# The six-layer stage of an eight-stage transformer kernel: scores of a unit put ahead of the previous unit's values on TensorE, and three norms applied by GpSimd

## Chip, core and metric

One NeuronCore of a Trainium2 chip runs the whole program in one launch. The metric is the device time of that launch in microseconds, taken over several executions. The kernel before takes 5420.99 us (median of 3; 5419.63 to 5421.79).

## What is computed

The input is `x` of 8 batches x 256 tokens x 128 features in fp32, with a condition vector per batch and a context of 64 tokens per batch. Eight blocks follow one another, each added to `x`. The change is in the fifth, which is six layers of this (16 heads of 8 features, feed-forward width 512):

```python
for i in range(6):
    xn = _adaln(x, noise_emb, n1_w[i], n1_b[i])          # layer norm, then a gain and a shift
    q, k, v = split(xn @ qkv_w[i].T); q, k = _rope(q), _rope(k)
    x = x + _attn(q, k, v, src_mask) @ so_w[i].T         # 256 keys
    xn = _adaln(x, noise_emb, n2_w[i], n2_b[i])
    q = _rope(xn @ cq_w[i].T); k = _rope(context @ ck_w[i].T); v = context @ cv_w[i].T
    x = x + _attn(q, k, v, ctx_mask) @ co_w[i].T         # 64 keys
    xn = _adaln(x, noise_emb, n3_w[i], n3_b[i])
    x = x + (gelu(xn @ f1_w[i].T + f1_b[i]) @ f2_w[i].T + f2_b[i])
```

where `_ln(x) = (x - m) * rsqrt(v + eps)` has the mean and variance of a token's 128 features. The part that the change moves to GpSimd is this subtraction and scaling.

## The kernel before

**The stage.** `dit_layers` keeps the tokens in SBUF as four pairs of batches (512 tokens, 4 tiles of 128). `course(slots)` runs one software-pipelined list of 26 **slots**; every pair in every layer is one slot for its own attention. In slot n the attention over the pair's own tokens runs, together with the cross attention of the pair of slot n-1, the feed-forward of the pair of slot n-2, and the norm, queries, keys and values of the pair of slot n+1. A slot without some of these is shorter: the first slot has no attention, the next two have no feed-forward, the last three end what is open. 21 slots have every part.

**The units.** A slot has 12 steps k = 0 to 11, each with one **unit** of attention: k = 0 to 7 are own units (one batch, four heads, 256 keys, so two exponentials of 128x1024), k = 8 to 11 are cross units (one exponential). A unit has

- group maxima: `max_scores(u, g)`, g = 0 to 3, bf16 matmuls (L1904 in the profile) into one of two PSUM banks used in turn; VectorE takes the row maximum of each (`row_max`, L2299), `turn_max` turns them on TensorE (L1916), and VectorE's `place_max` (L2317) makes the fp32 queries of the unit with the maximum in a spare feature;
- scores: `scores(u, 0)` and `scores(u, 1)` (L1942 own, L1946 cross) into PSUM banks 0 to 3;
- the exponentials on ScalarE (L2175), out of these banks into `probs`;
- values: `values(u)`, 8 matmuls (L1968 own, L1971 cross) into bank 4, which also make the sums; ScalarE copies the bank (`copy_values`, L2186), `turn_values` turns it on TensorE (L1980), and VectorE inverts the sums (L2329) and multiplies (L2339, `normalise`).

**The order.** There is no scheduler: each engine's program is written out, and engines wait for each other by semaphores. In step k of unit u TensorE does, outside the feed-forward's place (k = 7):

```python
values(u-1); scores(u, 0); max_scores(u+1, 2); scores(u, 1)
max_scores(u+1, 3); max_scores(u+2, 0); chain_early; turn_values(u-1)
turn_max(u+1); max_scores(u+2, 1); chain_late
```

`scores(u, 0)` waits for `queries_ready` of u (that is `place_max(u)`) and for all exponentials of u-1. `max_scores` waits until the row maximum of the group two places before it is taken, since there are two banks. `values(u-1)` waits for the exponentials of u-1 and for `normalise(u-2)`. VectorE does in the same step:

```python
row_max(u+1, 1); chain_early; row_max(u+1, 2); row_max(u+1, 3)
row_max(u+2, 0); chain_late; invert_sums(u-1); normalise(u-1); place_max(u+1)
```

ScalarE does `copy_values(u-1)`, the exponentials of u, `chain`. The `chain_early`, `chain_late` and `chain` functions hold the projections, norms and feed-forward of the neighbouring pairs, spread over the steps: on TensorE the turned norms (L1986), the 512-column projections (L1990) and by-token projections (L1994, L2007); on VectorE the statistics of a norm (`stats`, k = 0, 2 and 4, late in the last two), the applied norm (`apply`, L2354, four instructions in k = 1, 3 and 5, early), rotations (L2360) and residual sums (L2370). In step k = 7 TensorE does the four 512-column products of the feed-forward's first half (L2001) with `values(u-1)` between them, and the scores last.

GpSimd does the inverse roots of the norms (`root`, L2134 and L2137) and four sums a slot.

## Time and profile before

| What | Value |
|---|---|
| Runs | 5419.63, 5420.99, 5421.79 us |
| Span of the profiled execution, first to last instruction | 5413.8 us |
| Own time of the profiled execution, outside the profile | not recorded; the span is 7.2 us below the median of the runs |
| Granted TensorE clock, whole span | 0.918 of full speed |
| TensorE matmuls busy, of the span | 4614.7 us (85%) |
| VectorE busy | 2884.4 us (53%) |
| ScalarE busy | 2082.3 us (38%) |
| GpSimd busy | 576.5 us (11%) |
| The changed stage's exponentials | 2117.97 to 3915.2 us of the span |

The page gives busy time by engine over the whole program. The stage that the change touches lies in the middle third. A busy share does not say which engine sets the pace of a step, because TensorE's matmuls are pipelined and four of them share the array in most of these lines; the timeline and the words in its brackets (how long an engine was idle before an instruction, and which instruction ended that) do. In the timeline, instructions of one line are merged, so that "x3" and 1.95 us are three row maxima from the first start to the last end.

### The profile page before, as it was taken

Reading aid. Unit: us, or ns where it says so; the run is one execution under the profiler, and the core shown is the slowest. Engines: PE = TensorE matmul, PEld = TensorE weight load, DVE = VectorE, ACT = ScalarE, POOL = GpSimd, SP = SyncE. Lnnn points to the kernel's source line nnn. Section 1 sums busy time; section 2 is a strip of 40 time slices with the busy share of each in tenths; the row PEclk is TensorE's granted clock in tenths of the full one; section 3 lists DMA queues with packets and bytes.
Section 4 is the critical chain, followed back from the end, with each engine's and each line's share of the span. In section 5 each row is a group of like instructions: output and inputs, shape, how many; then the busy total and the mean of one; then the engine's idle time right before and its main releaser. Section 6 shows DMA issues by size and latency. Waiting matters only on the chain. (4 is left out here: it accounts for less than half of the span.)

```text
span 5413.8 us, 111310 instructions
## 1 busy us (share of the span) xinstructions
PE 4614.7 (85%) x45206; PEld 3112.5 (57%) x45501; DVE 2884.4 (53%) x9511; ACT 2082.3 (38%) x4120; POOL 576.5 (11%) x1302
## 2 busy tenths in 40 slices
PE   5489999999999965889989889899778979788784
PEld 3357777777777753555555555555444756566463
DVE  6634555555555535777766677666455224433433
ACT  2223333333333312665665666566433322212221
POOL 3300111111111112111111111111000000000000
PEclk8789999999999976999999999999889989878786
DMA  0000000000000011000000000000010010000000
GB/s 26 23 18 2 2 2 2 2 2 2 2 2 2 2 61 54 4 4 6 7 6 4 4 9 4 6 1 1 1 40 1 1 44 1 1 1 1 1 1 9
DMA packets 32272, 49.22 MB, mean 9 GB/s; under 512 B 8244, under 2 KB 23638, under 8 KB 31136
## 3 DMA queue, kind: packets, MB, share of 16 engines
q1 hardware_dynamic: 28448, 38.27, 2.2%
q8 instruction: 366, 6.00, 0.4%
q10 hardware_dynamic: 2304, 2.11, 0.1%
q0 software_dynamic: 1024, 1.78, 0.1%
q14 instruction: 130, 1.06, 0.1%
HBM read 37.72 MB, written 4.19 MB: 8 GB/s over the span
## 5 line engine op out<-in xcount | busy, mean ns | idle before, releaser
L2299 DVE TENSOR_REDUCE l_m<-psum 128x2 bf16<-128x512 f32 x768 | 503.8, 692 | 148.8 <-PE psum L1904 146.5
L2175 ACT ACTIVATE l_probs<-psum,l_mcol 128x1024 f32<-128x1024 f32 x384 | 406.3, 1109 | 159.2 <-PE psum L1942 159.2
L1184 PE MATMUL psum<-g_gx,ident 128*128 128x128 f32 x1536 | 416.0, 389 | 18.0
L1173 PE MATMUL psum<-g_still,ident_bf 128*128 128x256 bf16 (+3 forms) x1551 | 391.5, 281 | 1.7 <-PEq L58 1.7
L1904 PE MATMUL psum<-l_kb,l_qmb 32*128 32x256 bf16 x1536 | 295.4, 273 | 56.1 <-DVE l_m L2299 52.4
L1252 ACT ACTIVATE g_th<-g_pre 128x256 f32<-128x256 f32 x512 | 191.7, 417 | 314.3 <-DVE g_pre L1285 314.3
L1184 PEld LDWEIGHTS psum<-g_gx,ident 128*128 128x128 f32 x1536 | 279.4, 195 | 12.8
L1942 PE MATMUL psum<-l_qm,l_keys 32*128 32x256 f32 x3072 | 265.1, 418 | 13.3 <-issue 13.3
L2186 ACT COPY l_heads_out<-psum 128x256 f32<-128x256 f32 (+1 forms) x292 | 130.0, 445 | 369.8 <-PE psum L1968 186.3
L1285 DVE TENSOR_TENSOR g_pre<-g_encp,psum 128x256 f32<-128x256 f32 x512 | 192.8, 418 | 132.9 <-PE psum L1202 122.4
L2299 DVE TENSOR_REDUCE l_cm<-psum 128x4 bf16<-128x256 f32 x400 | 166.0, 427 | 179.8 <-PE psum L1904 179.6
L1968 PE MATMUL psum<-l_probs,l_v 128*32 128x256 f32 x3072 | 220.8, 408 | 46.7 <-DVE l_o L2339 29.1
L1187 PEld LDWEIGHTS psum<-g_shares,g_crows 128*128 128x128 f32 x1536 | 197.0, 189 | 78.9 <-issue 78.9
L1942 PEld LDWEIGHTS psum<-l_qm,l_keys 32*128 32x128 f32 x3072 | 180.5, 191 | 101.8 <-issue 94.1
L1173 PEld LDWEIGHTS psum<-g_still,ident_bf 128*128 128x128 bf16 x1808 | 224.3, 136 | 12.5 <-issue 2.3
L1187 PE MATMUL psum<-g_shares,g_crows 128*128 128x8 f32 x1536 | 212.8, 245 | 17.6
L1179 PE MATMUL psum<-g_encw,g_attnT 128*32 128x128 f32 x6144 | 220.8, 277 | 0.0
L3430 ACT ACTIVATE l_probs<-psum 128x1024 f32<-128x1024 f32 x80 | 81.9, 1023 | 326.1 <-PE psum L3257 228.7
L1904 PEld LDWEIGHTS psum<-l_kb,l_qmb 32*128 32x128 bf16 x1536 | 112.1, 93 | 164.0 <-DVE l_m L2299 75.2
L1256 ACT COPY g_crows<-psum 128x128 f32<-128x128 f32 x256 | 67.9, 265 | 348.3 <-PE psum L1179 348.3
L1270 POOL TENSOR_SCALAR g_kept<-g_zh 128x8 f32<-128x8 f32 x256 | 59.6, 233 | 1321.2 <-DVE g_zh L1311 1321.2
L1179 PEld LDWEIGHTS psum<-g_encw,g_attnT 128*32 128x32 f32 x6144 | 152.2, 109 | 67.7 <-DVE g_attnT L1293 67.7
(567 smaller groups left out, 9761.9 us busy)
## 6 DMA issues: line engine op xcount, KB each, us to landing
s_w<-in_S_w SPq DMA_DIRECT2D x16, 256.0 KB, 5.0
f_w<-in_F_w SPq DMA_DIRECT2D x2, 2048.0 KB, 12.5
l_wf<-in_L_W SPq DMA_DIRECT2D x6, 576.0 KB, 3.8
l_w<-in_L_W SPq DMA_DIRECT2D x1, 3072.0 KB, 10.6
l_nw<-in_L_nw SPq DMA_DIRECT2D x1, 2304.0 KB, 8.0
l_wc<-in_L_W SPq DMA_DIRECT2D x6, 384.0 KB, 3.0
h_w<-in_H_W ACTq DMA_DIRECT2D x16, 129.0 KB, 3.0
h_w<-in_H_W SPq DMA_DIRECT2D x16, 129.0 KB, 3.0
```

Of the source, the lines that this page charges most:

```text
L1173: pe.matmul(psum[:, bank, 0:cols], cst["ident_bf"][:], still[:, 0:cols], start=True, stop=True)
L1179: last = pe.matmul(psum[32 * p:32 * p + 32, bank, 0:D], attnT[:, 2 * p:2 * p + 32], encw[:, p, gate, :], start=True, stop=True)
L1184: pe.matmul(psum[:, bank, 0:P], cst["ident"][:], repeated(gx(gate, s)), start=True, stop=False)
L1187: pe.matmul(psum[:, bank, 0:B], crows[:, i, :], shares[:], start=False, stop=True)\
L1252: act.activation(th[:, i, :, :], pre[:, i, :, :], ACT.Tanh).then_inc(sig["tanh_ready"], 1)
L1285: dve.tensor_tensor(pre[:, i, :, :], encp[:, i, :, :], query[:, i, :].unsqueeze(2).to_broadcast([P, PAIRS, C]), ALU.add)\
L1904: last = pe.matmul(psum[:, bank, x.width * t:x.width * (t + 1)], queries, far_keys, start=True, stop=True)
L1942: last = pe.matmul(psum[:, g, S * part:S * part + S], keys[group(g), s.buf, x.j % 2, S * x.b + P * part:S * x.b + P * part + P], qm[group( ...
L1968: last = pe.matmul(psum[group(g), VALUES, 0:S], v[:, s.buf, 2 * x.b + part, GROUP * g + x.j, :], probs[:, u % 2, part, S * g:S * g + S], s ...
L2175: act.activation(probs[:, u % 2, chunk, :].rearrange("p (g n) -> p g n", g=GROUP), psum[:, 0:GROUP, S * chunk:S * chunk + S], ACT.Exp, bia ...
L2186: act.copy(heads_out[:, u % 2, 0:cols], psum[:, VALUES, 0:cols]).then_inc(sig["values_copied"], 1)
L2299: dve.tensor_reduce(place, psum[:, c.bank(("max", u, g)), 0:x.tiles * x.width] .rearrange("p (t k) -> p t k", t=x.tiles), AX.X, ALU.min)\
```

## The change

On TensorE `values(u-1)` goes from the front of a step to a place behind `scores(u, 1)`, in all steps but k = 7. On ScalarE `exponentials(u, 0)` goes ahead of `copy_values(u-1)`, so that the copy stands between an own unit's two exponentials, and behind a cross unit's only one. The three `apply` calls leave VectorE; GpSimd makes them directly behind its inverse root, with a wait until the previous contents of the buffer have been turned.

```diff
                             else:
-                                values(done)
                                 scores(u, 0)
                                 max_scores(after, 2)
                                 scores(u, 1)
+                                values(done)
                                 max_scores(after, 3)
                                 max_scores(later, 0)
                                 chain_early(s, i, k)
...
+                def apply(pool, n, w, pair, done, dst):
+                    pool.wait_ge(sig[n + "_rstd_ready"], done + 1)
+                    if done:
+                        pool.wait_ge(sig[n + "_turned"], done)
+                    for t in range(PT):
+                        last = pool.tensor_scalar(dst[:, t, :], Y[:, PT * pair + t, :], w["mv"][:, t, 0:1],
+                                                  w["rstd"][:, t, :], ALU.subtract, ALU.mult)
+                    last.then_inc(sig[n + "_normed"], 1)
...
                             root(pool, "n2", n2, nx)
+                            apply(pool, "n2", n2, s.mid_pair, nx, xn[1])
...
                             root(pool, "n1", n1, nn)
+                            apply(pool, "n1", n1, s.next_pair, nn, xn[0])
...
                             root(pool, "n3", n3, nf)
+                            apply(pool, "n3", n3, s.late_pair, nf, xn[2])
...
                             if u is not None:
+                                exponentials(u, 0)
                                 if not (k == FF_PLACE and s.ff):
                                     copy_values(c.behind(u))
-                                exponentials(u, 0)
                                 if units[u].own:
                                     exponentials(u, 1)
...
                         if k == 1 and s.context:
-                            apply("n2", n2, s.mid_pair, nx, xn[1])
...
-                        if k == 3 and s.following:
-                            apply("n1", n1, s.next_pair, nn, xn[0])
...
-                        if k == 5 and s.ff:
-                            apply("n3", n3, s.late_pair, nf, xn[2])
```

TensorE, the second own step of the first slot with attention (k = 1): `l_probs,l_v` are the values, `l_qm,l_keys` the scores, `l_kb,l_qmb` the group maxima.

```order
 L2058 MATMUL psum<-l_wc,l_ctxT 128x128
-L1968 MATMUL psum<-l_probs,l_v 32x256 x8
-L1942 MATMUL psum<-l_qm,l_keys 128x256 x4
-L1904 MATMUL psum<-l_kb,l_qmb 128x256 x2
-L1942 MATMUL psum<-l_qm,l_keys 128x256 x4
+L1942 MATMUL psum<-l_qm,l_keys 128x256 x4
+L1904 MATMUL psum<-l_kb,l_qmb 128x256 x2
+L1942 MATMUL psum<-l_qm,l_keys 128x256 x4
+L1968 MATMUL psum<-l_probs,l_v 32x256 x8
 L1904 MATMUL psum<-l_kb,l_qmb 128x256 x4
 L1980 MATMUL psum<-ident,l_heads_out 128x128 x2
```

The values have passed the scores, and now stand between them and four group-maximum matmuls (those of group 3 of the next unit and of group 0 of the one after).

TensorE, the first cross step (k = 8) of the same slot: here the projection of the next pair's values (`l_wa,l_xn1T`) stands between the group maxima and the turned values (`ident,l_heads_out`, outside the piece).

```order
 L1990 MATMUL psum<-l_xn1T,l_wa 128x512
-L1968 MATMUL psum<-l_probs,l_v 32x256 x8
-L1946 MATMUL psum<-l_qm,l_ckeys 64x256 x4
-L1904 MATMUL psum<-l_ckb,l_cqmb 128x64 x4
-L1946 MATMUL psum<-l_qm,l_ckeys 64x256 x4
+L1946 MATMUL psum<-l_qm,l_ckeys 64x256 x4
+L1904 MATMUL psum<-l_ckb,l_cqmb 128x64 x4
+L1946 MATMUL psum<-l_qm,l_ckeys 64x256 x4
+L1968 MATMUL psum<-l_probs,l_v 32x256 x8
 L1904 MATMUL psum<-l_ckb,l_cqmb 128x64 x8
 L1994 MATMUL psum<-l_wa,l_xn1T 128x128 x4
```

The same move, and the turned values of this step are behind the values, two groups and the projection.

GpSimd, one slot with feed-forward, as it stands with the change: `l_xn<-l_y` are the applied norms (L2144), and every other row was there before in this order.

```order
L2134 TENSOR_SCALAR l_n_veps<-l_n_mv 128x4
L2137 TENSOR_TENSOR l_n_rstd<-l_n_veps,mhalf 128x4
L2144 TENSOR_SCALAR l_xn<-l_y,l_n_mv,l_n_rstd 128x128 x4
L2162 TENSOR_TENSOR l_cqT<-l_tc 128x512
L2134 TENSOR_SCALAR l_n_veps<-l_n_mv 128x4
L2137 TENSOR_TENSOR l_n_rstd<-l_n_veps,mhalf 128x4
L2144 TENSOR_SCALAR l_xn<-l_y,l_n_mv,l_n_rstd 128x128 x4
L2168 TENSOR_TENSOR l_y<-l_y,l_constf 128x512
L2173 TENSOR_TENSOR l_qT<-l_t 128x512
```

The four instructions of each norm went in behind the inverse root; nothing else of this queue changed its place.

## Rows read from the trace of the kernel before

**Rows 1.** the page: its line of the span

```profile
span 5413.8 us, 111310 instructions
```

**Rows 2.** the timeline, ScalarE: exponentials; start us, us, engine line op out<-in xcount [idle before <-releaser]

```profile
2242.94 2.12 ACT L2175 ACTIVATE l_probs<-psum,l_mcol 128x1024 f32<-128x1024 f32 x2 [0.70 <-PE psum L1942]
...
2387.84 2.12 ACT L2175 ACTIVATE l_probs<-psum,l_mcol 128x1024 f32<-128x1024 f32 x2 [0.70 <-PE psum L1942]
...
2397.87 2.12 ACT L2175 ACTIVATE l_probs<-psum,l_mcol 128x1024 f32<-128x1024 f32 x2 [0.91 <-PE psum L1942]
...
2404.05 2.12 ACT L2175 ACTIVATE l_probs<-psum,l_mcol 128x1024 f32<-128x1024 f32 x2 [0.91 <-PE psum L1942]
...
2421.29 2.12 ACT L2175 ACTIVATE l_probs<-psum,l_mcol 128x1024 f32<-128x1024 f32 x2 [0.90 <-PE psum L1942]
...
2437.43 1.11 ACT L2175 ACTIVATE l_probs<-psum,l_mccol 128x1024 f32<-128x1024 f32 x1 [1.03 <-PE psum L1946]
...
2442.16 1.11 ACT L2175 ACTIVATE l_probs<-psum,l_mccol 128x1024 f32<-128x1024 f32 x1 [0.82 <-PE psum L1946]
...
2460.28 2.12 ACT L2175 ACTIVATE l_probs<-psum,l_mcol 128x1024 f32<-128x1024 f32 x2 [0.70 <-PE psum L1942]
...
3788.01 2.12 ACT L2175 ACTIVATE l_probs<-psum,l_mcol 128x1024 f32<-128x1024 f32 x2 [0.70 <-PE psum L1942]
```

**Rows 3.** the timeline of the second own step of a slot, all engines

```profile
2390.58 1.07 PE L1968 MATMUL psum<-l_probs,l_v 128*32 128x256 f32 x16
...
2391.58 0.92 PE L1942 MATMUL psum<-l_qm,l_keys 32*128 32x256 f32 x10
...
2392.13 0.27 PE L1904 MATMUL psum<-l_kb,l_qmb 32*128 32x256 bf16 x1
...
2392.54 1.95 DVE L2299 TENSOR_REDUCE l_m<-psum 128x2 bf16<-128x512 f32 x3 [0.31 <-PE psum L1904]
...
2392.67 0.38 PE L1904 MATMUL psum<-l_kb,l_qmb 32*128 32x256 bf16 x2
...
2393.38 0.37 PE L1904 MATMUL psum<-l_kb,l_qmb 32*128 32x256 bf16 x2 [0.34 <-DVE l_m L2299]
...
2394.40 0.20 DVE L2329 RECIPROCAL l_rsum<-psum 128x8 f32<-128x8 f32 x1
...
2394.78 0.47 DVE L2317 SCALAR_TENSOR_TENSOR l_qm<-l_qT,l_narrow,psum 128x256 f32<-128x256 f32 x1
...
2395.45 1.07 PE L1968 MATMUL psum<-l_probs,l_v 128*32 128x256 f32 x16
```

**Rows 4.** the timeline, VectorE, fifth own step: the statistics of a norm, and an applied norm

```profile
2411.50 0.86 DVE L2345 BATCH_NORM_STATS2 l_n_stats<-l_y 128x6 f32<-128x128 f32 x4
...
2412.70 0.18 DVE L2329 RECIPROCAL l_rsum<-psum 128x8 f32<-128x8 f32 x1
...
2414.20 1.12 DVE L2354 TENSOR_SCALAR l_xn<-l_y,l_n_mv,l_n_rstd 128x128 f32<-128x128 f32 x4
```

**Rows 5.** the timeline around the eighth step and the ninth

```profile
2437.59 1.16 PE L1994 MATMUL psum<-l_wa,l_xn1T 128*128 128x128 f32 x8
...
2439.01 0.21 DVE L2329 RECIPROCAL l_rsum<-psum 128x8 f32<-128x8 f32 x1 [0.62 <-PE psum L1980]
...
2439.39 0.74 DVE L2317 SCALAR_TENSOR_TENSOR l_qm<-l_cqT,l_narrow,psum 128x512 f32<-128x512 f32 x1
```

**Rows 6.** the timeline of the first step of the course: queries placed, scores behind them

```profile
2114.89 0.47 DVE L2317 SCALAR_TENSOR_TENSOR l_qm<-l_qT,l_narrow,psum 128x256 f32<-128x256 f32 x1
...
2115.41 1.65 PE L1942 MATMUL psum<-l_qm,l_keys 32*128 32x256 f32 x10
```

**Rows 7.** groups of instructions of GpSimd, shapes apart: busy us, mean ns | idle before us

```profile
L2146 POOL TENSOR_TENSOR l_ckT<-l_tk 128x128 f32<-128x128 f32 x25 | 11.3, 454 | 85.6 <-DVE l_tk L2360 85.6
```

**Rows 8.** windows: us, busy and (x) of PE, PEld, DVE, ACT, POOL, PEclk, DMA, GB/s

```profile
2387.80:2460.30 72.50, 65.03 (x679) 37.96 (x678) 51.92 (x136) 45.07 (x64) 9.23 (x12) 1.00 0.03 7
...
2912.90:2920.80 7.90, 6.84 (x51) 3.01 (x50) 6.16 (x21) 3.78 (x7) 1.21 (x2) 0.78 0.00 0
```

More of the change, by code:

```diff
@@ L2349, in stats @@
                         last.then_inc(sig[n + "_var_ready"], 1)
-                    def apply(n, w, pair, done, dst):
-                        dve.wait_ge(sig[n + "_rstd_ready"], done + 1)
-                        for t in range(PT):
-                            last = dve.tensor_scalar(dst[:, t, :], Y[:, PT * pair + t, :], w["mv"][:, t, 0:1],
-                                                     w["rstd"][:, t, :], ALU.subtract, ALU.mult)
-                        last.then_inc(sig[n + "_normed"], 1)
                     def rotated(projected, done, table, first, cols, dst, name=None):
```

## The prediction

> **What bounds the kernel now.** The page gives one profiled execution with a span of 5413.8 us [rows 1], 7.2 us under the median of the runs; I work out a difference from that execution and add it to the median. Its shares of busy time name TensorE, but they do not say what ends a step, so the views I use are the starts of the exponentials, which give the length of each step, and then the timeline of single steps with the words on idle time.
>
> A full slot runs from exponential to exponential in 2460.28 - 2387.84 = 72.44 us [rows 2], and TensorE is busy in 65.03 of such 72.50 us at full clock [rows 8]: at most 7.5 us a slot are idle. From 2242.94 to 3788.01 lie 21 full slots and 1545.07 us, while 21 x 72.44 is 1521.2. The 24 us over it are steps at a lower granted clock: the window of one such step 2 is 7.90 us long with a clock of 0.78 (a mean over it of TensorE's two levels, 1.2 and 2.4 GHz) [rows 8], where the same step takes 2404.05 - 2397.87 = 6.18 us undisturbed [rows 2]. What ends an undisturbed step is seen in the second own step [rows 3]: values start at 2390.58, scores 1.00 later at 2391.58, the group maximum inside them at 2392.13; VectorE starts three row maxima at 2392.54, 0.96 after the scores began, and is done with them and at the inversion at 2394.40; 0.38 later it places the next queries, which takes 0.47. The next values start at 2395.45. So the loop is values, scores, exponentials or row maxima, values. The placed queries are ready at 2395.25, 1.2 us before the next scores start (values 1.00 behind 2395.45): they have slack, because values stand between them and the scores.
>
> **What the change removes and adds.** Count every time from the start S of a unit's scores.
>
> *Values behind the scores.* The 1.00 us before S goes from the loop. In its place the values take TensorE from S+1.09 (2392.67 - 2391.58 [rows 3]) to S+2.09. Behind them stands the group maximum 3, which used to start at S+1.09. VectorE needs 0.41 from its start to the row maximum (2392.13 to 2392.54), so it begins the third row maximum at S+2.50, where it now is at S+1.58, right behind the one before. Two row maxima of 0.6 bring it to S+3.70. Then come the late vector work of the step, 0.38 from inversion to placing, 0.47 of placing, and 0.05 until the scores start (2114.89 + 0.47 to 2115.41 [rows 6]). **The new floor of an own step is 4.60 us plus the late vector work**, and nothing stands between placing and scores any more. The exponentials are not what waits longest: they begin 1.42 after the scores (2397.87 against 2395.45 + 1.00) and take 2.12 [rows 2, 3], so even with a copy of 0.5 between them they end at S+4.04. The turned values are shorter too in an own step: their copy ends by S+3.0, and turning takes less than half a microsecond. So the values leave one loop and delay another by almost as much.
>
> *Step by step.* (Durations without a group are from the same timeline, one slot of it.) Own steps 0 and 1: TensorE's late projection or turn ends them, at 5.09 and 4.80; together 9.89 against 2397.87 - 2387.84 = 10.03 [rows 2]: -0.14. Step 2: late statistics of 1.20 (2411.50 to 2412.70 [rows 4]), less 0.03 of inversion gap: 5.77. Step 3: the second cross query projection starts at S+2.71, its rotation frees the bank 1.85 later, and the by-token projection of 1.08 follows: 5.70. Step 4: statistics again, 5.77. Step 5: a rotation that ends the vector chain 1.45 after its start at S+3.88: 5.38. Together 22.62 against 2421.29 - 2397.87 = 23.42 [rows 2]: -0.80. Steps 6 and 7: the key projection waits for a rotation that comes 0.59 later than now, and the feed-forward behind it is TensorE work back to back, so +0.59; then the scores of step 8 need only the exponentials of step 7, where now the 1.00 of values stands behind the same event: -0.41 together. Step 8: values to S+2.40 (cross scores take 1.40), two maxima 0.29, the value projection 1.00, turned values; the inversion came 1.42 after that projection began (2437.59 to 2439.01 [rows 5]), so now at S+4.11; placing 0.38 later takes 0.74; scores at 5.28, against 2442.16 - 2437.43 = 4.73 [rows 2]: +0.55. Step 9: two halves of the feed-forward keep TensorE busy throughout, and moving 1.00 us inside it changes nothing. Step 10 has step 8's pattern: +0.57. Step 11: residual sum and placing behind a projection that starts 1.00 later, less the values: +0.25. Sum: -0.14 - 0.80 - 0.41 + 0.55 + 0.57 + 0.25 = **+0.02 us a slot, under +1 us over 21**.
>
> *The norms.* VectorE loses 12 instructions a slot, 1.12 us for each four [rows 4]. They stand early in steps 1, 3 and 5. Under the new order VectorE has 0.9 us idle before the third row maximum, so what goes there goes from idle time; only step 3 would have been late by 0.2 with it, and 5.70 already has it out. GpSimd's price is not in the trace: from below VectorE's 0.28 an instruction (1.12 for four), from above its two-input sum of the same size, 0.454 [rows 7], so 1.1 to 1.8 us for four; I take 1.8, the same engine. TensorE reads the tightest of the three, the third norm, some 4.2 us after its inverse root is ready, so 1.8 is hidden, and twice that would be. Nothing is queued behind it on GpSimd that is wanted soon. Uncovered it is only in the first slot and the last two, where no attention runs: three times 0.4 to 0.7, about +1.2. On this the Trainium skill speaks against the change: its page "GPSIMD Engine Reference", section "Engine selection", puts elementwise work on VectorE and calls GpSimd about twice as slow for two inputs, near line rate for one. The trace agrees in direction, 0.454 on GpSimd [rows 7] against 0.28 on VectorE [rows 4] for the same size, and by that rule the sum would stay as it is, since the work is covered.
>
> *The ends.* Two slots without feed-forward lose the gains of steps 2 and 7 and lose 0.9 in step 9, whose turned values no longer hide behind anything: +1.4 each, +2.9. The last three cross steps outside full slots: +1.5.
>
> Total: 0.4 + 1.2 + 2.9 + 1.5 = +6 on 5421.0: **5427 us, no change within 0.2%** (0.2%, 11 us, is about what a measurement of this kernel tells from no change).
>
> **Bounds.** The 0.05 between placing and scores may be 0.15, as between a row maximum (ended 2393.23) and the group maximum behind it (2393.38 [rows 3]); with six such steps a slot that is 0.6 x 21 = +13 us. Values behind scores instead of behind other matmuls could overlap by 0.05 or cost 0.07, their last drain (1.07 against 1.00): -6 to +9 in the same steps. I keep 0.05 and 1.00, the rows of those same instructions.
>
> **Rivals.**
>
> *A, faster by the clock (0.17).* The 24 us of low clock [rows 2, 8] lie in steps 2 and 4 of some slots. There TensorE waits longest; the new order shortens steps 2 and 3 by 0.8 together. If the clock then stays up: 5427 - 24 = 5403 us. Against it: step 4 still has 1.5 us of wait.
>
> *B, the loop pays in full (0.06).* If the row maxima were not the next bound and each full slot lost half of its 7.5 idle us, it would be 5421 - 21 x 3.7 = 5343. I do not believe in it since the two banks forbid it; half of that, 5380, if values and group maxima overlap.
>
> *C, slower by the clock (0.16).* Steps 8, 10 and 11 get a wait of about 1 us each, where TensorE now has next to none. A low-clock step costs about 7.9 - 6.2 = 1.7 us; if one more falls in every second slot, 21 x 0.5 x 1.7 = +18, so 5445 us. It decides once the granted clock drops in cross steps. The Trainium skill's page "TensorE: Matmul & The Clock Gate", section "HAM oscillation — how this bites in real kernels", says that repeated waits throttle TensorE again and again; here that would give this rival its time.
>
> *D, slower by hand-over (0.18).* The 0.15 above instead of 0.05, or the values' 0.07: 5427 + 13 = 5440 us. What decides is the time from placing to scores.
>
> That the change does not do what it says is excluded by the listed order on both engines.
>
> **How the numbers follow.** The forecast holds 0.43. Faster is A and B, 0.23; slower is C and D, 0.34, and same is 0.43. The predicted time is 5427. The range goes from A, 5403, rounded to 5402, to above C with D's half, 5450: it leaves out B and the case that C and D both hold, under 0.2.
>
> **What would show it.** In the changed profile: step lengths near 5.8 in steps 2 and 4, 5.3 in steps 8 and 10, and 15.6 for 6 and 7 together; scores whose wait is ended by the placed queries (the place where now values wait for the exponentials or the normalised output); VectorE idle 0.9 before the third row maximum; GpSimd busier by 80 to 130 us (73 norms at 1.1 to 1.8) with no TensorE wait on it except at the ends. It is wrong if own steps other than 6 fall below 4.6, if scores wait for exponentials in most steps, or if the clock in the stage's window is not near 0.97.

## The result, and the profile after

| | Before | After |
|---|---|---|
| Median of 12 runs each | 5421.14 us (5398.09 to 5440.68) | 5432.78 us (5425.10 to 5458.32) |
| Ratio to before, runs on the same chip compared | | 1.0038 (1.0023 to 1.0053) |
| Span of the profiled execution | 5413.8 us | 5425.1 us |
| First to last exponential of the stage | 1796.1 us | 1820.3 us |

The ratio is that of executions at the faster of two speeds; of all executions in this document one, of e4 below (6022.59 us at a granted clock of 0.712), was at the slower and is left out.

The change makes the kernel slower by 0.38%. The time lies inside the range that was given, but the sign is not that of the likeliest case, which was no change within 0.2%. By the medians the loss is 11.6 us, by the ratio, which compares runs on the same chip, 20.6 us; the stage itself, from its first exponential to its last, lost 24.2 us in the profiled execution. The rest of the profile is not touched by the change and moved by itself: behind the stage 1499.7 us before and 1484.1 us after, and between 1478 and 1505 us over the eleven kernels measured here. So below I judge each kernel by the stage and by the ratio, and take neither from a single span.

The page after: its span, busy times and four of its groups.

```profile
span 5425.1 us, 111380 instructions
...
PE 4591.5 (85%) x45206; PEld 3065.6 (57%) x45501; DVE 2809.6 (52%) x9219; ACT 2064.2 (38%) x4120; POOL 805.0 (15%) x1594
...
L2311 DVE TENSOR_REDUCE l_m<-psum 128x2 bf16<-128x512 f32 x768 | 515.9, 692 | 251.1 <-PE psum L1904 249.7
...
L1942 PE MATMUL psum<-l_qm,l_keys 32*128 32x256 f32 x3072 | 265.2, 415 | 86.3 <-DVE l_qm L2329 72.3
...
L1904 PE MATMUL psum<-l_kb,l_qmb 32*128 32x256 bf16 x1536 | 243.4, 280 | 25.9 <-DVE l_m L2311 24.4
...
L2144 POOL TENSOR_SCALAR l_xn<-l_y,l_n_mv,l_n_rstd 128x128 f32<-128x128 f32 x292 | 229.3, 798 | 7.6
```

Both parts of the change are to be seen. GpSimd has 229.3 us of applied norms, 798 ns each, and TensorE's own scores (L1942) now sit idle for the placed queries (the line numbers of ScalarE, and of VectorE up to the place where it applied the norm, are 12 higher than before: placing is L2329, inversion L2341, exponentials L2187; behind that place they are 5 higher, rotations L2365). VectorE is less busy, 2809.6 us against 2884.4, and waits more for the group maxima of own units (251.1 us, where it was 148.8). The view of the line of the own scores gives their idle times, of weight loads and matmuls together, and how often each cause ended one:

```profile
its engine sat idle before it (us, times) until:
  DVE l_qm L2329: 189.1, 192
  issue: 32.7, 51
```

The starts of the exponentials give the steps, as before [rows 2]. These are of one slot with the clock up throughout:

```profile
2399.83 1.11 ACT L2187 ACTIVATE l_probs<-psum,l_mcol 128x1024 f32<-128x1024 f32 x1 [2.64 <-PE psum L1942]
...
2410.06 1.11 ACT L2187 ACTIVATE l_probs<-psum,l_mcol 128x1024 f32<-128x1024 f32 x1 [0.28 <-PE psum L1942]
...
2416.05 1.11 ACT L2187 ACTIVATE l_probs<-psum,l_mcol 128x1024 f32<-128x1024 f32 x1 [2.34 <-PE psum L1942]
...
2449.05 1.11 ACT L2187 ACTIVATE l_probs<-psum,l_mccol 128x1024 f32<-128x1024 f32 x1 [1.68 <-PE psum L1946]
...
2454.27 1.11 ACT L2187 ACTIVATE l_probs<-psum,l_mccol 128x1024 f32<-128x1024 f32 x1 [1.64 <-PE psum L1946]
...
2472.66 1.11 ACT L2187 ACTIVATE l_probs<-psum,l_mcol 128x1024 f32<-128x1024 f32 x1 [2.64 <-PE psum L1942]
```

The slot takes 2472.66 - 2399.83 = 72.83 us, where it took 72.44: +0.39, with +0.02 forecast. Step 2 is 2416.05 - 2410.06 = 5.99, step 8 is 2454.27 - 2449.05 = 5.22. The table has the undisturbed lengths of all steps, in us, of the kernels that matter most (the experiments e2, e3 and e8 come below):

| Step | 0 | 1 | 2 | 3 | 4 | 5 | 6+7 | 8 | 9 | 10 | 11 | slot |
|---|---|---|---|---|---|---|---|---|---|---|---|---|
| before | 5.16 | 4.88 | 6.18 | 6.04 | 5.61 | 5.59 | 16.15 | 4.72 | 7.70 | 4.83 | 5.59 | 72.44 |
| forecast | 5.09 | 4.80 | 5.77 | 5.70 | 5.77 | 5.38 | 15.74 | 5.28 | 7.70 | 5.40 | 5.84 | 72.47 |
| after | 5.25 | 4.97 | 5.99 | 5.75 | 5.99 | 5.42 | 15.84 | 5.22 | 7.47 | 5.27 | 5.65 | 72.83 |
| e3 | 5.06 | 4.49 | 5.57 | 5.72 | 5.50 | 5.39 | 15.84 | 5.43 | 7.68 | 5.48 | 5.86 | 72.01 |
| e8 | 5.06 | 4.49 | 5.57 | 5.72 | 5.51 | 5.39 | 15.84 | 5.06 | 7.69 | 4.76 | 5.86 | 70.94 |

Where the forecast failed is seen in one own step with the clock up, all engines (some instructions left out):

```profile
2403.67 0.92 PE L1942 MATMUL psum<-l_qm,l_keys 32*128 32x256 f32 x10
...
2404.42 0.61 PE L1942 MATMUL psum<-l_qm,l_keys 32*128 32x256 f32 x5
...
2404.96 1.07 PE L1968 MATMUL psum<-l_probs,l_v 128*32 128x256 f32 x16
...
2405.96 0.39 PE L1904 MATMUL psum<-l_kb,l_qmb 32*128 32x256 bf16 x4
...
2406.39 1.30 DVE L2311 TENSOR_REDUCE l_m<-psum 128x2 bf16<-128x512 f32 x2 [0.95 <-PE psum L1904]
...
2407.59 0.20 DVE L2341 RECIPROCAL l_rsum<-psum 128x8 f32<-128x8 f32 x1
...
2407.96 0.47 DVE L2329 SCALAR_TENSOR_TENSOR l_qm<-l_qT,l_narrow,psum 128x256 f32<-128x256 f32 x1
...
2408.64 0.92 PE L1942 MATMUL psum<-l_qm,l_keys 32*128 32x256 f32 x10
...
2412.57 0.86 DVE L2357 BATCH_NORM_STATS2 l_n_stats<-l_y 128x6 f32<-128x128 f32 x4
...
2414.11 0.47 DVE L2329 SCALAR_TENSOR_TENSOR l_qm<-l_qT,l_narrow,psum 128x256 f32<-128x256 f32 x1
...
2414.64 0.92 PE L1942 MATMUL psum<-l_qm,l_keys 32*128 32x256 f32 x10 [0.46 <-DVE l_qm L2329]
...
2415.34 3.14 POOL L2144 TENSOR_SCALAR l_xn<-l_y,l_n_mv,l_n_rstd 128x128 f32<-128x128 f32 x4
```

The scores start at S = 2403.67. The values start at 2404.96, S+1.29, and end for the next instruction at 2405.96, S+2.29. I had them at S+1.09 and S+2.09, since the group maximum 3 stood at S+1.09 in that place before [rows 3]. The row maxima therefore start at 2406.39, S+2.72 instead of S+2.50. From there everything is as forecast: the inversion 1.20 later, placing 0.37 behind it, and, in the next step, behind its own placing, scores at 2414.64, 0.06 after the end of placing (2414.11 + 0.47). The values themselves cost 1.00, as before.

The granted clock is the other part. Windows over this slot, and over one step 5 that fell low:

```profile
2399.83:2472.66 72.83, 64.31 (x682) 36.48 (x682) 48.87 (x124) 44.11 (x63) 18.63 (x23) 1.00 0.03 7
```

```profile
2500.60:2508.20 7.60, 7.60 (x51) 3.72 (x50) 3.59 (x9) 4.06 (x6) 3.72 (x5) 0.58 0.00 0
```

The first window has TensorE at 2.4 GHz throughout. In the second the mean granted clock is 0.58, so most of it ran at 1.2 GHz, and the step took 2508.64 - 2500.90 = 7.74 us instead of 5.42; TensorE was busy all the time. What TensorE did before it fell is in the first of these rows, a wait of 1.53 us for placed queries in step 4; the second is the same instruction in the undisturbed slot, where the clock stayed up behind the same wait:

```profile
2499.21 0.92 PE L1942 MATMUL psum<-l_qm,l_keys 32*128 32x256 f32 x10 [1.53 <-DVE l_qm L2329]
...
2426.37 0.92 PE L1942 MATMUL psum<-l_qm,l_keys 32*128 32x256 f32 x10 [1.53 <-DVE l_qm L2329]
```

Added up over the 21 full slots, 71.7 us lie at the low level, where it was 51.2 us; after, it falls late in step 4 of 16 slots and lasts into step 5, where it was in step 2 of six and step 4 of nine. The five slots without it are every fourth, from the 3rd to the 19th, so the fall comes in a fixed order; what sets that order no run tells.

The 24.2 us of the stage come out as: 21 slots with 0.39 each, +8.2; low clock in them, +6.0 (1559.26 against 1545.06 us for the 21, less 8.2); the slots ahead of them +5.5; those behind them +4.5. The clock's part is of one execution each.

### The profile page after: what moved, and what is told of

It reads as the page before. It is cut to its first block and busy times, and to the rows that moved or that the text cites. A ratio compares the mean times of both kernels' runs of the same rounds, so it can differ in the third digit from the quotient of the medians.

```text
span 5425.1 us, 111380 instructions
## 1 busy us (share of the span) xinstructions
PE 4591.5 (85%) x45206; PEld 3065.6 (57%) x45501; DVE 2809.6 (52%) x9219; ACT 2064.2 (38%) x4120; POOL 805.0 (15%) x1594
## 5 line engine op out<-in xcount | busy, mean ns | idle before, releaser
L2311 DVE TENSOR_REDUCE l_m<-psum 128x2 bf16<-128x512 f32 x768 | 515.9, 692 | 251.1 <-PE psum L1904 249.7
L2187 ACT ACTIVATE l_probs<-psum,l_mcol 128x1024 f32<-128x1024 f32 x384 | 426.1, 1116 | 295.9 <-PE psum L1942 295.9
L1942 PE MATMUL psum<-l_qm,l_keys 32*128 32x256 f32 x3072 | 265.2, 415 | 86.3 <-DVE l_qm L2329 72.3
L1904 PE MATMUL psum<-l_kb,l_qmb 32*128 32x256 bf16 x1536 | 243.4, 280 | 25.9 <-DVE l_m L2311 24.4
L1942 PEld LDWEIGHTS psum<-l_qm,l_keys 32*128 32x128 f32 x3072 | 177.7, 187 | 147.8 <-DVE l_qm L2329 116.8
L2144 POOL TENSOR_SCALAR l_xn<-l_y,l_n_mv,l_n_rstd 128x128 f32<-128x128 f32 x292 | 229.3, 798 | 7.6
L2187 ACT ACTIVATE l_probs<-psum,l_mccol 128x1024 f32<-128x1024 f32 x100 | 111.4, 1114 | 254.4 <-PE psum L1946 254.4
L3430 ACT ACTIVATE l_probs<-psum 128x1024 f32<-128x1024 f32 x80 | 81.9, 1024 | 309.1 <-PE psum L3257 228.7
```

The source lines that it names most:

```text
L1904: last = pe.matmul(psum[:, bank, x.width * t:x.width * (t + 1)], queries, far_keys, start=True, stop=True)
L1942: last = pe.matmul(psum[:, g, S * part:S * part + S], keys[group(g), s.buf, x.j % 2, S * x.b + P * part:S * x.b + P * part + P], qm[group( ...
L2144: last = pool.tensor_scalar(dst[:, t, :], Y[:, PT * pair + t, :], w["mv"][:, t, 0:1], w["rstd"][:, t, :], ALU.subtract, ALU.mult)
L2187: act.activation(probs[:, u % 2, chunk, :].rearrange("p (g n) -> p g n", g=GROUP), psum[:, 0:GROUP, S * chunk:S * chunk + S], ACT.Exp, bia ...
L2311: dve.tensor_reduce(place, psum[:, c.bank(("max", u, g)), 0:x.tiles * x.width] .rearrange("p (t k) -> p t k", t=x.tiles), AX.X, ALU.min)\
```

## The experiments

Each kernel is the changed one or the one before with one edit. In diffs the places are those of the quoted order of TensorE, ScalarE and VectorE. The summary first; "low clock" is the time at the lower level in the 21 full slots, "stage" is first to last exponential, both of one profiled execution, and the ratio is to the kernel before. The low clock of one execution is not the order's alone: before and e1 have the same slot and differ by 10 us in it, e3, e7 and e8 have the same steps 0 to 5 and 13.7, 20.5 and 30.7 us, and the mean granted clock of 31 executions of the kernel before on one chip lay between 0.914 and 0.926. So differences of 10 or 20 us in that column tell nothing.

| Kernel | Slot, us | Low clock, us | Stage, us | Ratio |
|---|---|---|---|---|
| before | 72.44 | 51.2 | 1796.1 | 1 |
| after | 72.83 | 71.7 | 1820.3 | 1.0038 (1.0023 to 1.0053) |
| e1 norms alone | 72.45 | 61.4 | 1808.0 | 1.0007 (0.9986 to 1.0028) |
| e2 order alone | none undisturbed | 88.7 | 1833.3 | 1.0064 (1.0040 to 1.0087) |
| e3 group maximum 3 ahead of the values | 72.01 | 13.7 | 1781.9 | 0.9956 (0.9935 to 0.9977) |
| e4 placing early | 72.80 | 0 | 1779.6 | 0.9975 (0.9951 to 0.9998) |
| e5 copy ahead of exponentials | 73.30 | 81.9 | 1838.3 | 1.0098 (1.0065 to 1.0131) |
| e6 before, placing early | 78.0 | 150.2 | 1968.7 | 1.0296 (1.0258 to 1.0335) |
| e7 e3, placing early in four steps | 71.59 | 20.5 | 1770.2 | 0.9933 (0.9912 to 0.9954) |
| e8 e7, turned maxima first | 70.94 | 30.7 | 1751.1 | 0.9919 (0.9893 to 0.9946) |
| e9 e3 with norms on VectorE | 72.50 | 58.0 | 1807.0 | 1.0007 (0.9987 to 1.0026) |

### e1: the norms alone

The kernel before, with the three `apply` calls on GpSimd:

```diff
                             root(pool, "n2", n2, nx)
+                            apply(pool, "n2", n2, s.mid_pair, nx, xn[1])
...
-                            apply("n2", n2, s.mid_pair, nx, xn[1])
```

(and the same for `n1` and `n3`.) What was expected:

> The kernel before with only the norms made by GpSimd. Theory H (order: values put in front of a group maximum hold up VectorE's third row maximum; the norms are covered): a full slot without low clock stays at 72.44 us from exponential to exponential, and the only loss is at the three or four places where no attention covers a norm, 3.2 us for four on GpSimd against 1.1 on VectorE, so +6 to +8 us, ratio 1.001. Theory G (GpSimd: its instructions of 0.80 us come late for TensorE or hold up VectorE): the slot goes to 72.8 us and the ratio to 1.003 or more.

The ratio is 1.0007, no difference that can be told, and the undisturbed slot stays at 72.45. In the old order nothing on VectorE's side of steps 1, 3 and 5 ends a full step, so taking 3.4 us a slot from it gives nothing. GpSimd's four instructions take nearly three times what VectorE's took, and in the full slots that costs nothing either: the view of the line of the applied norm, who waited for it, has four waits in the whole program, all outside the full slots. These are the kernel before's and the changed kernel's (e1 has 36.4 in its four):

```profile
  PEld psum L1986: 28.6, 4
```

```profile
  PEld psum L1986: 36.5, 4
  PE psum L1986: 35.7, 4
```

So at these four places it costs 7.8 us, the +6 to +8 expected, which the ratio is too wide to show.

### e2: the order alone

The kernel before, with the new order on TensorE and ScalarE and the norms left on VectorE:

```diff
-                                values(done)
                                 scores(u, 0)
                                 max_scores(after, 2)
                                 scores(u, 1)
+                                values(done)
                                 max_scores(after, 3)
...
+                                exponentials(u, 0)
                                 if not (k == FF_PLACE and s.ff):
                                     copy_values(c.behind(u))
-                                exponentials(u, 0)
```

> The kernel before with only the new order on TensorE and ScalarE; the norms stay on VectorE. H: a full slot without low clock takes 72.8 to 73.0 us (step 3 may lose 0.2 more, since the norm stands in front of its second row maximum), steps 8, 10 and 11 as in the changed kernel, and the time is 12 to 16 us over before, ratio 1.0025. G: the slot is back at 72.4 and the time within 5 us of before.

The ratio is 1.0064, above the 1.0025 expected and above the whole change's 1.0038; the two intervals overlap a little, so that the order alone costs more than the whole change rests on the steps. These are the changed kernel's but for two things. Step 3 takes 6.15 instead of 5.75, where the applied norm stands on VectorE ahead of the rotation that the step waits for; and all 21 slots have low clock in steps 4 and 5 (88.7 us in sum), so no undisturbed slot is left and the mean is 75.09. So the loss is the order's, and GpSimd's norms take back the 0.40 us of step 3 in each slot; what they do to the clock this pair does not tell. They are worth nothing in the old order and something in the new one.

### e3: group maximum 3 ahead of the values

If the dearer place of the values is what failed the forecast, then the group maximum 3 in its old place gives most of it back:

```diff
                                 scores(u, 1)
-                                values(done)
                                 max_scores(after, 3)
+                                values(done)
                                 max_scores(later, 0)
```

> The changed kernel with the maximum of group 3 put back behind the scores, ahead of the values. H: VectorE's third row maximum follows the second at once (0.62 later, against about 1.7), its fourth starts about 0.5 us earlier, and own steps 2 and 4 go from 5.99 to about 5.5 us, steps 0 and 1 lose about 0.2 each; steps 8, 10 and 11 stay. A slot of about 71.5 us, 25 us under the changed kernel, ratio to before 0.999 or less. Rival T (turned values: the copy, turn and inversion are what placing waits for in own steps): no own step gets more than 0.1 us shorter.

This kernel is faster than both, 0.9956. The timeline of an own step:

```profile
2327.27 0.92 PE L1942 MATMUL psum<-l_qm,l_keys 32*128 32x256 f32 x10
...
2328.14 0.31 PEld L1904 LDWEIGHTS psum<-l_kb,l_qmb 32*128 32x128 bf16 x2
...
2328.36 0.38 PE L1904 MATMUL psum<-l_kb,l_qmb 32*128 32x256 bf16 x2
...
2328.66 0.59 PEld L1968 LDWEIGHTS psum<-l_probs,l_v 128*32 128x32 f32 x16 [0.21 <-issue]
...
2328.66 1.07 PE L1968 MATMUL psum<-l_probs,l_v 128*32 128x256 f32 x16
...
2329.67 0.39 PE L1904 MATMUL psum<-l_kb,l_qmb 32*128 32x256 bf16 x2
...
2330.09 0.70 DVE L2311 TENSOR_REDUCE l_m<-psum 128x2 bf16<-128x512 f32 x1 [0.56 <-PE psum L1904]
```

Behind the scores, which start at S = 2327.27, the group maximum begins at S+1.09, and the values behind it at S+1.39. So of the 0.30 that the group maximum takes, the values pay only 0.10: for the other 0.20 they would have waited in any case. The forms in the rows say what differs: scores and group maxima are 32 rows by 128 columns of the array (32\*128), values are 128 rows by 32 columns (128\*32). That 0.20 belongs to a change of form is my reading. It fits the cross steps, where the scores are 32\*64 and what follows changes form in any case: the group maximum before and the values after both start 1.40 behind them (rows in the account below). The rows do not tell it from another reading, that the weights could not be loaded ahead: the group maximum's load starts 0.22 before its matmul (2328.14), the values' load only with the matmul (2328.66). No run tells the two apart. The Trainium skill, page "TensorEngine Tiling (Array Packing)", section "Key Properties", says that changing the tiling mode drains TensorE; these rows agree, and if the reading holds the drain costs 0.20 us behind fp32 scores.

The larger gain is on VectorE. Only one row maximum is left behind the values, starting at S+2.82, instead of two from S+2.72; step 2 goes from 5.99 to 5.57, step 1 from 4.97 to 4.49. Cross steps, which I had expected to stay, are longer by 0.2 each (5.43, 7.68, 5.48, 5.86); there the group maxima stand ahead of the values and what follows them. So the slot is 72.01, not the 71.5 expected. The low clock is 13.7 us, in four slots, and the granted clock over all ten executions has a mean of 0.923, where the kernel before beside them has 0.919. Why it stays up is not shown: the longest wait for placed queries, in step 4, is 1.48 us, where it was 1.53.

### e4: placing early in every step

The other way to shorten the path from group maxima to scores is to place the queries before the vector work of the neighbouring pairs, which no unit waits for:

```diff
                             row_max(later, 0)
+                            place_max(after)
                             chain_late(s, i, k)
                             invert_sums(done)
                             normalise(done)
-                            place_max(after)
```

> The changed kernel with VectorE placing the next queries right behind its fourth row maximum, ahead of the late vector work and of the inversion and the normalised output. H, with the second half of my account (placing stands at the end of VectorE's step and now starts the scores): steps 2, 4, 8, 10 and 11 shorten by 0.5 to 1.2 us each, to what TensorE's own work or the exponentials allow (about 4.3 to 4.6 without extra TensorE work), the slot goes to 69 to 70 us, ratio to before 0.987 to 0.992. Rival P (TensorE's own work is the floor of nearly every step): under 1 us a slot, ratio 1.000 or more.

The expected 69 to 70 us a slot did not come. The ratio is 0.9975, and in the profiled execution the stage is the shortest but those of e7 and e8, though the undisturbed slot is 72.80, as in the changed kernel: there is no low clock at all in the full slots, and the granted clock of the nine executions has a mean of 0.925. What steps 2, 4, 8, 10 and 11 gain (5.46, 4.45, 5.07, 5.00, 4.95) is lost in steps 0, 3, 5 and 6+7 (6.03, 6.38, 6.41, 16.56), where TensorE waits for the work that now stands behind placing:

```profile
2343.79 0.66 PE L1986 MATMUL psum<-ident,l_xn 128*128 128x128 f32 x4 [0.97 <-POOL l_xn L2144]
...
2349.62 1.12 PE L1990 MATMUL psum<-l_xn1T,l_wa 128*128 128x512 f32 x2 [0.96 <-DVE l_t L2365]
```

The first row is the third norm that GpSimd applies: its statistics come later by the placing, and its 3.1 us are covered no more. The view of the applied norm's line, who waited for it, has 26 waits where the changed kernel has 4:

```profile
  PEld psum L1986: 64.0, 26
```

So GpSimd's norms hang on their cover; with it gone they cost what their length says.

### e5: the copy ahead of the exponentials

ScalarE's part of the change taken back, TensorE's kept:

```diff
                             if u is not None:
-                                exponentials(u, 0)
                                 if not (k == FF_PLACE and s.ff):
                                     copy_values(c.behind(u))
+                                exponentials(u, 0)
```

> The changed kernel with ScalarE's order undone: it copies the values of the previous unit ahead of the first exponential again, while TensorE makes them behind the scores. The copy then waits for the values (their end 2.36 us after the scores' start S), so an own unit's exponentials run from S+2.8 to S+4.9 and not from S+1.4 to S+3.9. If VectorE's placing (S+4.9 without late work) is what starts the scores, as H says, the steps that carry late statistics or rotations hardly change and only those with work on ScalarE between exponentials and a TensorE product (2, 6) get longer: slot 74 us, ratio 1.007 to 1.010. Rival X (the exponentials start the scores): every own step 0.9 us longer, slot 79 us, ratio 1.025.

1.0098. In the new order of TensorE the values end after the scores, so a copy in front holds the exponentials back. The undisturbed slot is 73.30, +0.47 on the changed kernel: +0.48 in step 2 (6.47) and +0.22 in step 8 (5.44), -0.21 in step 0 (5.04). The low clock is 81.9 us. The two halves of the reordering belong together.

### e6: the kernel before, placing early

The edit of e4 in the kernel before.

> The kernel before with VectorE placing the next queries ahead of late work, inversion and normalised output. In the order of before the values stand ahead of the scores and wait for the normalised output, so placed queries have slack and what is behind the placing has none: H expects no step to get shorter and steps 4, 8, 10 and 11 to get 0.3 to 0.7 longer; slot 74 us or more, ratio 1.005 to 1.012. If placing had been on the path before too (rival Q), the slot falls under 72.4.

The direction was as expected, the size was not: 1.0296, 78.0 us a slot (one slot alone is undisturbed) and 150.2 us of low clock. Steps 8, 10 and 11 grew by 0.9 to 1.0, and steps 3, 5 and 6+7, where I had expected nothing, by 0.7. The views of two lines name much of it, the cross values' for the normalised output and the 512-column projections' for rotations; these are of e6, and the kernel before has 22.9 and 23.2 us in the same 52 waits:

```profile
  DVE l_co L2339: 70.0, 52
```

```profile
  DVE l_t L2360: 56.2, 52
```

In the old order placing had slack, since values stood between it and the scores. Moving it ahead delays rotations and normalised output and buys nothing. This tells the two orders apart: early placing is a loss where it has slack and a gain where scores wait for it.

### e7: placing early where nobody waits for the late vector work

Built on e3, in the steps 2, 8, 9 and 10 alone:

```diff
                             row_max(later, 0)
+                            if k in (2, 8, 9, 10):
+                                place_max(after)
                             chain_late(s, i, k)
                             invert_sums(done)
                             normalise(done)
-                            place_max(after)
+                            if k not in (2, 8, 9, 10):
+                                place_max(after)
```

> Group maximum 3 ahead of the values, norms on GpSimd, and placing first only in steps 2, 8, 9 and 10, where no rotation that TensorE waits for and no statistics of the tight third norm are put behind it. H: steps 2, 8 and 10 at about 5.45, 5.1 and 5.1 us, all others as with the maximum alone (5.72, 5.50, 5.39 in steps 3 to 5); slot 71.1 us, ratio 0.991 to 0.994. If moving the placing shifts as much elsewhere, as it did when it was done in all steps, the slot stays at 72.0.

0.9933, and 71.59 us a slot. The ratio alone does not tell it from e3; the slot does. All of the gain on e3 is in steps 8 and 10 (5.28 and 5.22 against 5.43 and 5.48); step 2, where I had expected 5.45, stays at 5.57, so late statistics are not what ends it in e3. Step 8 shows what is left, TensorE and one VectorE row:

```profile
2371.31 1.16 PE L1994 MATMUL psum<-l_wa,l_xn1T 128*128 128x128 f32 x8
...
2372.30 0.38 PE L1980 MATMUL psum<-ident,l_heads_out 128*128 128x128 f32 x2
...
2372.52 0.39 PE L1916 MATMUL psum<-ident_bf,l_cm 128*128 128x128 bf16 x4
...
2372.95 0.75 DVE L2329 SCALAR_TENSOR_TENSOR l_qm<-l_cqT,l_narrow,psum 128x512 f32<-128x512 f32 x1 [1.10 <-PE psum L1916]
...
2373.75 0.66 PE L1946 MATMUL psum<-l_qm,l_ckeys 32*64 32x256 f32 x8 [0.62 <-DVE l_qm L2329]
```

Placing waits for the turned maxima (L1916), which stand behind the turned values (L1980).

### e8: the turned maxima first in cross steps

```diff
                                 chain_early(s, i, k)
-                                turn_values(done)
+                                if k < OWN:
+                                    turn_values(done)
                             turn_max(after)
+                            if k >= OWN:
+                                turn_values(done)
```

> The same with TensorE turning the next maxima ahead of the previous unit's values in the cross steps. H: placing no longer waits for the turned values there, steps 8 and 10 shorten by another 0.3 to 0.4 us, slot 70.5 us, ratio 0.989 to 0.993. If TensorE's work fills those steps already, nothing changes against the run before.

The same place, in e8 (the line of placing is L2332 here):

```profile
2367.10 1.16 PE L1994 MATMUL psum<-l_wa,l_xn1T 128*128 128x128 f32 x8
...
2368.09 0.39 PE L1916 MATMUL psum<-ident_bf,l_cm 128*128 128x128 bf16 x4
...
2368.32 0.39 PE L1980 MATMUL psum<-ident,l_heads_out 128*128 128x128 f32 x2
...
2369.32 0.45 PE L1946 MATMUL psum<-l_qm,l_ckeys 32*64 32x256 f32 x4 [0.40 <-DVE l_qm L2332]
```

From the start of the projection to the scores it is 2369.32 - 2367.10 = 2.22 us, where e7 has 2373.75 - 2371.31 = 2.44. Steps 8 and 10 fall to 5.06 and 4.76, the slot to 70.94. The ratio is 0.9919, 5370.08 us against 5419.28 us of the kernel before in the same comparison. It is the fastest version measured; its distance to e7 is inside both intervals, and it rests on the slot (0.65 us, 21 times) and the stage (19 us).

### e9: the good order, with the norms on VectorE

e2 with e3's edit, which leaves the norms' place as the only difference from e3.

> Group maximum 3 ahead of the values, as in the third run, but with the norms left on VectorE: what the GpSimd half is worth under the better order. The first norm stands in front of VectorE's second row maximum in step 3, which has least room there: H says step 3 goes from 5.72 to about 6.1 us, as it went from 5.75 to 6.15 under the changed order, steps 1 and 5 stay within 0.1, slot 72.4 us against 72.01, and about 5 us come back at the uncovered ends; ratio to before 0.995 to 0.999. Rival (the norms on VectorE fill idle time here as well): slot 72.0 us and a ratio of 0.994 or less.

1.0007 against e3's 0.9956. The undisturbed slot is 72.50, 0.49 above e3's: 0.36 in step 3 (6.08 against 5.72) and 0.13 in step 1 (4.62 against 4.49). The low clock is 58.0 us instead of 13.7, and the granted clock over all executions has a mean of 0.920 instead of 0.923. So in this order GpSimd's norms are worth 0.5% of the kernel: about 10 us of it is 21 x 0.49, and the rest goes with the clock.

## Why the prediction was right or wrong

**What bounds a step: right.** Own scores wait for placed queries and for almost nothing else (192 idle times, 189.1 us), where before own values waited for exponentials (58.5 us) or for the normalised output (29.1 us).

**The new floor of an own step: the step that failed.** "In its place the values take TensorE from S+1.09 (2392.67 - 2391.58) to S+2.09". They take it from S+1.29 to S+2.29. I put the start of one instruction, a group maximum, down for another in the same place. That was in the text as a bound, "or cost 0.07", and as half of rival D, but the bound came from a drain behind values and not from a change behind scores, and was three times too small. It makes steps 2 and 4 longer than forecast by 0.22; that the 0.16 and 0.17 of steps 0 and 1 are the same 0.20 is likely and not shown. e3 shows the place (S+1.09 for the group maximum, S+1.39 for the values behind it).

**The 0.05 from placing to scores: right**, 0.06 in the row above. Rival D's first half is out.

**Single steps.** 3 and 5 were 0.05 and 0.04 longer than forecast, 6 and 7 together 0.10. Step 9 was forecast unchanged, "moving 1.00 us inside it changes nothing", and became 0.23 shorter; steps 8, 10 and 11 came out 0.06 to 0.19 under the forecast. In cross steps the values began at S+1.40 as I had it. These rows are of the eighth step, before and then after:

```profile
2435.90 0.66 PE L1946 MATMUL psum<-l_qm,l_ckeys 32*64 32x256 f32 x8
...
2437.30 0.36 PE L1904 MATMUL psum<-l_ckb,l_cqmb 32*128 32x64 bf16 x8
```

```profile
2447.51 0.66 PE L1946 MATMUL psum<-l_qm,l_ckeys 32*64 32x256 f32 x8 [0.82 <-ACT l_probs L2187]
...
2448.91 1.07 PE L1968 MATMUL psum<-l_probs,l_v 128*32 128x256 f32 x16
```

So that 1.40 too was the start of a group maximum (2437.30 - 2435.90), taken for that of the values, the same slip as in own steps. That it came out right is luck: there the two start alike. Own steps missed by +0.96 a slot, cross steps gave back 0.61, and 0.35 is left, times 21: 7.4 us.

**The norms: mechanism right, price wrong.** "1.1 to 1.8 us for four; I take 1.8". They take 3.14 to 3.2 us, 798 ns each, above my upper end, which was GpSimd's two-input sum of the same size at 454 ns [rows 7]. The cover held, as "twice that would be" said. The Trainium skill, page "GPSIMD Engine Reference", section "Engine selection", has one-input work on GpSimd near line rate; here four took 2.8 times VectorE's 1.12 us [rows 4], and one took more than the two-input sum, so for this form the measurement decides against that rule. What I had too low is what the offload would give: step 3 had 0.2 us for it and got 0.40 (e2 against the changed kernel), and under the better order of e3 0.5% of the kernel with the clock (e9).

**The ends: too low.** Forecast 1.2 + 2.9 + 1.5 = 5.6 us; the slots ahead and behind took 5.5 + 4.5 = 10.0, and the first exponential came 2.7 later. Of these, 2.1 are the first norm, covered by nothing (from its statistics to the turned norm it is 5.99 us, where it was 3.87), and 0.6 was there before it. The norms are the term that was mis-sized: their four waits grew by 36.5 - 28.6 = 7.9 us, where I had 1.2. Three of the four lie behind the full slots and grew by 5.9, more than the 4.5 there, so my +1.5 for the last cross steps did not come. Ahead of the full slots the clock was low for 10.8 us, where it was 6.0; how the rest of the 5.5 divides is not shown.

**The clock: right in kind, wrong in place.** Rival C had low clock in steps 8, 10 and 11 for +18 us. It came in own steps 4 and 5, and is 6.0 us in the sum of the changed kernel's execution, which is no more than executions of one kernel differ by: the granted clock over all of its twelve has a mean of 0.918, and the kernel before in e1's comparison 0.919. A, the clock staying up, did not come with this change, but it is real: e3 and e4 have it, 13.7 and 0 us, and means of 0.923 and 0.925. The Trainium skill's page "TensorE: Matmul & The Clock Gate", section "HAM oscillation — how this bites in real kernels", tells of a kernel that is throttled again by each of its repeated waits. Its waits are for a DMA and 3 to 5 us long; here the fall comes behind a wait of 1.53 us in step 4, so the rows agree in kind and not in size, and what that page's case would give rival C's waits of about 1 us, which no low clock followed, is open. The same wait of 1.53 us stands in the undisturbed slot, so which step falls, and in which slots, I can't derive from the rows: e2 and the changed kernel have the same steps but for 0.40 us in step 3, and 21 slots fall in one and 16 in the other. That stays open.

**The chances.** Same had 0.43 and slower 0.34, and slower came. With the measured sizes in its own terms the sum becomes 5427 + 7.4 for the steps + 4.4 for the ends + 6.0 for the clock = 5445 us, or 5447 with the first norm; the ratio gives 5420.99 x 1.0038 = 5441.6. Without the clock it would still be 5439, slower by more than 0.2%, so the mis-sized start of the values and the ends decide the sign.

## What to carry to other kernels

When an instruction is moved on TensorE, take its start in the new place from a row in which an instruction of the same form stands behind the same neighbour, and not from whatever stood there: behind scores the group maximum began at S+1.09 and the values at S+1.29. A reordering that takes work out of one loop pays only if what then ends the loop is moved up as well: the same change cost 0.4% by itself and gave 0.8% with the group maximum, four placings and the turned maxima put in front of the work that nobody waited for. An offload that is worth nothing under one order (e1) can be worth 0.5% under another (e9 against e3), so the two are to be measured together, and its cover is to be looked at again after each reordering (e4).

## What the runs showed of the hardware that was not expected

- Matmuls of the form 128\*32 behind fp32 ones of the form 32\*128 started 0.20 us later than bf16 ones of the form 32\*128 did in that place.
- GpSimd's subtraction and scaling of 128x128 fp32 with two operands per partition took 798 ns, against 454 ns for its sum of two 128x128 tiles; VectorE's instructions showed no slowing beside it (in the changed kernel a row maximum at 2403.22, with GpSimd at such a norm throughout, took 0.69 us, and their mean before is 692 ns).
- With one wait of 1.53 us in a slot of 73 us, 16 of 21 slots had low clock right behind it and 5 had none. Over the eleven kernels the low clock lay between 0 and 150.2 us in 21 slots, and a clean slot that was 0.79 us longer (e4 against e3, 72.80 and 72.01) went with a shorter stage, 1779.6 against 1781.9 us, in the two profiled executions; by the ratio e3 is the lower of the two, within both intervals.
- Unchanged code behind the stage took 1478 to 1505 us from profile to profile.
